# Differential attention with a routed expert before and after it: the short tile's shift of the differences from POOL to DVE

## What is computed

```python
q, k, v = rope(xn @ Wq), rope(xn @ Wk), xn @ Wv      # 16 query heads, 4 key heads
energy = einsum('bqhad,bkhad->bahqk', q, k)          # causal mask: -1e30
scores = softmax(energy / sqrt(D))
diff = scores[:, 0] - lam * scores[:, 1]             # lam: one number per head
diff = softmax(where(causal, NEG, diff))
att = einsum('bhqv,bvhd->bqhd', diff, v)
att = att * rsqrt(mean(att * att) + EPS) * rms_w * (1 - LAM_INIT)
x = x + att @ Wo
```

## Time and profile before

| | |
|---|---|
| three executions | 2122.12, 2129.94, 2130.46 us, median 2129.94 |
| profiled execution | 2123.43 us |
| its span, first to last instruction | 2121.7 us |
| PE busy | 1555.5 us (73%) |
| DVE busy | 1467.3 us (69%) |
| ACT busy | 1219.2 us (57%) |
| POOL busy | 1057.3 us (50%) |
| granted TensorE clock, mean over the span | 0.838 |

### The profile page before, as it was taken

The page is one execution under the profiler, slowest core; times in us unless marked ns, Lnnn a source line. Parts: engine busy times, 40 slices in busy tenths (PEclk is TensorE's granted clock), DMA queues, the critical chain, the costliest instruction groups (busy, mean ns, idle before and its releaser), DMA issues. The chain is left out here.

```text
span 2121.7 us, 44318 instructions
## 1 busy us (share of the span) xinstructions
PE 1555.5 (73%) x10713; PEld 1091.9 (51%) x10713; DVE 1467.3 (69%) x4351; ACT 1219.2 (57%) x3332; POOL 1057.3 (50%) x1477
## 2 busy tenths in 40 slices
PE   0579814347888888988888888888888888886521
PEld 0355402125666666666666666666666566763221
DVE  5774431127887888888888888888888776751167
ACT  0121102126887878887888887788878776761100
POOL 0220003225666667767766777767677565552200
PEclk9999956666878999899999999999999877676655
DMA  3330271111111111111111121111111100000084
GB/s 122 94 87 0 67 245 30 41 39 33 24 28 36 41 48 43 38 51 47 45 48 38 43 52 43 49 43 38 49 48 42 40 20 20 15 15 30 35 324 158
DMA packets 183784, 122.58 MB, mean 58 GB/s; under 512 B 140225, under 2 KB 140609, under 8 KB 183746
## 3 DMA queue, kind: packets, MB, share of 16 engines
q1 hardware_dynamic: 183746, 122.15, 19.6%
HBM read 57.07 MB, written 33.55 MB: 43 GB/s over the span
## 5 line engine op out<-in xcount | busy, mean ns | idle before, releaser
L1185 ACT ACTIVATE ex<-bank,nbias 128x512 f32<-128x512 f32 (+3 forms) x1024 | 527.8, 534 | 141.2 <-DVE nbias L902 140.7
L895 DVE TENSOR_REDUCE nmax<-bank 128x2 f32<-128x1024 f32 (+3 forms) x448 | 340.7, 795 | 29.9 <-PE bank L1331 29.5
L1361 PEld LDWEIGHTS bank<-vs,pr 128*128 128x128 f32 x2560 | 343.2, 210 | 17.8 <-issue 13.4
L1361 PE MATMUL bank<-vs,pr 128*128 (+1 forms) x2560 | 343.4, 286 | 7.2 <-issue 4.1
L1329 PE MATMUL bank<-ks,qs 96*128 (+2 forms) x1024 | 271.8, 342 | 95.7 <-ACT ex L1185 94.2
L1343 PE MATMUL bank<-cst,df 128*128 128x128 f32 x1280 | 274.5, 319 | 88.8 <-ACT pr L1202 88.5
L1081 POOL TENSOR_SCALAR ex<-ex,gam 128x128 f32<-128x128 f32 (+3 forms) x512 | 313.4, 623 | 0.0
L1202 ACT ACTIVATE pr<-bank 128x128 f32<-128x128 f32 (+3 forms) x512 | 233.0, 455 | 70.5 <-PE bank L1343 70.1
L927 DVE CUSTOM_DVE_ANT_0 df<-ex 128x128 f32<-128x128 f32 (+3 forms) x512 | 263.3, 529 | 9.7 <-issue 4.9
L1343 PEld LDWEIGHTS bank<-cst,df 128*128 128x128 f32 x1280 | 174.1, 171 | 117.9 <-ACT pr L1202 101.6
L1185 ACT ACTIVATION_READ_ACCUMULATOR ex<-bank,nbias 128x1 f32 x1024 | 216.6, 212 | 0.0
(11 more groups left out here) (215 smaller groups left out, 3164.0 us busy)
## 6 DMA issues: line engine op xcount, KB each, us to landing
qs<-turned SPq DMA_DIRECT2D x384, 64.0 KB, 2.2
xs<-in_x SPq DMA_DIRECT2D x64, 256.0 KB, 3.0
x_dram<-y SPq DMA_DIRECT2D x32, 256.0 KB, 3.8
b_xs<-x_dram SPq DMA_DIRECT2D x32, 256.0 KB, 2.6
x<-x_dram SPq DMA_DIRECT2D x32, 256.0 KB, 2.7
x_dram<-x SPq DMA_DIRECT2D x32, 256.0 KB, 2.0
y_dram<-scratch SPq DMA_DIRECT2D x32, 256.0 KB, 2.0
c_x<-x_dram SPq DMA_DIRECT2D x8, 1024.0 KB, 13.6
```

The lines of the kernel that those rows point to most:

```text
L895: ins = dve.tensor_reduce(nmax[:, j, i, :], energy(j, i), X, ALU.max, negate=True)
L1185: ac.activation(ex[j % 4][:, a, lo:hi], energy(j, i)[:, a, :], ACT.Exp, bias=nbias[:, j, i, a:a + 1], scale=reg, accum_out=esum[:, j, i, a ...
L1361: mm = pe.matmul(bank[:, 7, t * DV:(t + 1) * DV], pr[j % 2][:, lo + k * P:lo + (k + 1) * P], val, start=(k == 0), stop=(k == t))
```

## The change

The short tile's shift is taken from POOL's program and put into DVE's, for the same pair as the bias that DVE has just made (lag 4 for both), so a step earlier than POOL had it. In DVE's group the bias of the difference now goes ahead of gamma, and the shift comes behind gamma. POOL's mask is now the first thing of its step. PE's and ACT's programs are unchanged.

```diff
@@ DVE
+                def shift(at):
+                    j = at.j
+                    dbias_done.wait(dve, at.units(1))
+                    lo, hi = span(j, 0)
+                    dve.tensor_scalar(df[j % 4][:, lo:hi], df[j % 4][:, lo:hi], rsum[:, j, 0, 0:1],
+                                      dbias[:, j, 0:1], ALU.mult, ALU.add).then_inc(shifted_short.sem, 1)
...
-                            [(1, inv_sums), (1, gamma), (4, diff_bias), (3, difference(0))],
+                            [(1, inv_sums), (4, diff_bias), (1, gamma), (4, shift), (3, difference(0))],
@@ POOL
-                def shift(at):
-                    j = at.j
-                    dbias_done.wait(gp, at.units(1), apart_p)
-                    lo, hi = span(j, 0)
-                    gp.tensor_scalar(df[j % 4][:, lo:hi], df[j % 4][:, lo:hi], rsum[:, j, 0, 0:1],
-                                     dbias[:, j, 0:1], ALU.mult, ALU.add).then_inc(shifted_short.sem, 1)
...
-                run_bodies(gp, [[(5, shift)], [(2, mask), (2, scale)], []],
+                run_bodies(gp, [[], [(2, mask), (2, scale)], []],
```

More of the change, by code:

```diff
@@ L879, in _ @@
             def _(dve):
-                for s in (st_done, ve_done, xn_done, st2_done, ve2_done, xn2_done, rope_v, max_done, bias_done, rs_done, gam_done, diff_done, dbias_done, att_out,
+                for s in (st_done, ve_done, xn_done, st2_done, ve2_done, xn2_done, rope_v, max_done, bias_done, rs_done, gam_done, diff_done, dbias_done, shifted_short, att_out,
                           ss_done, s2_done, de_done, an_done, x2_done, lg_out):
@@ L1063, in _ @@
             def _(gp):
-                for s in (rstd_done, rstd2_done, rope_done, masked, scaled, shifted_short, sq_done, ri_done, lo_done,
+                for s in (rstd_done, rstd2_done, rope_done, masked, scaled, sq_done, ri_done, lo_done,
                           rlo_done, al_done, lo2_done):
```

## The result

| | before | after |
|---|---|---|
| median of 4 executions | 2126.03 us (2121.51 to 2130.46) | 2168.44 us (2164.25 to 2172.32) |
| profiled execution, its span | 2123.43, 2121.7 us | 2164.25, 2162.5 us |
| granted clock over the span | 0.838 | 0.83 |

The ratio is 1.0199 [1.0165, 1.0233]: slower by 2%, 42 us. The forecast was 2139 with a range of 2121 to 2159; the result lies above that range.

What follows compares the result with a forecast made beforehand. No engine was full, so a chain between engines was taken as the bound. Terms of +0.40 us in 22 turns (8.8) plus 1.0 in ten others gave +9.8 us, on the median 2139.7, stated as 2139, range 2121 to 2159.

Steps and rivals of the forecast that it cites:

- The bound: Steady attention loop: no engine is full; a chain going round between engines sets turns of 45.06 us.
- The price of the shift: On DVE: 0.31 us on 128 columns and 0.39 on 256, 88 us of busy time for 256 shifts.
- DVE's wait of 2.44 us: DVE's wait for PE at 1112.05, covering groups beside the chain; expected to fall to under 2 us.
- Term 1: DVE's group at 1085.24, on the chain: shift added, partly filling gaps; +0.10 us a turn, bounds 0 and 0.38.
- no idle time before gamma: Sign in the profile after: the bias of the difference fills DVE's 0.31 us idle before gamma at 1085.24.
- Term 2: After the power, POOL's earlier scaling meets DVE's long difference at 1091.79: +0.15 us a turn, bounds 0 and 0.59.
- Term 3: DVE's group at 1115.12, nearly on the chain: shift and one more turn-taking, +0.15 us a turn, bounds 0 and 0.75.
- Term 4: Gains from a lighter POOL at DVE's delays at 1084.35 and 1081.98: 0 us a turn, bounds -0.45 and +0.3.
- Turn-taking everywhere: Rival: every added DVE operation waits for one POOL instruction; 1.72 us a turn, 2168, halfway 2153; chance 0.15.
- The power did not block the shift: Rival claimed the opposite: DVE's shift cannot start during POOL's 2.92 us power, head norm 0.43 us later; 2154, chance 0.07.
- The lighter POOL: Rival: DVE's stalls behind POOL at 1081.98 and 1084.35 vanish, -0.45 us in 32 turns, 2116; chance 0.16.

Runs made afterwards that it cites:

- runs 5: The changed kernel with POOL's first rotary addition one place earlier, ahead of step 2's mask and scalings: 2135.09 us, ratio 1.0011.
- run 11: The changed kernel with one tiny memset (0.1 us) added on POOL ahead of the first rotary addition: 2139.11 us, ratio 1.0058.
- run 9: The kernel before with a DVE reduction over 256 constants ahead of step 2's bias of the exponentials: 2149.69 us, ratio 1.0105.
- run 2: The changed kernel with gamma ahead of the bias of the difference again, shift still on DVE: 2181.62 us, ratio 1.0209.
- run 10: The changed kernel with the bias of the exponentials in accumulator form and POOL's first rotary addition one place earlier: 2102.54 us, ratio 0.9871.
- run 12: The changed kernel unaltered, measured again on the chip of the last lot, against the kernel before: 2165.92 us, ratio 1.0179.
- run 4: The changed kernel without the short shift anywhere, DVE only raising the semaphore, and gamma's product made a comparison: 2125.12 us, ratio 0.9977.
- run 6: The changed kernel with the bias of the exponentials in the form that also writes a sum: 2102.63 us, ratio 0.9854.

## Why the prediction was wrong

- **The bound** was read rightly: a chain with turns of 45 us, on which the bias of the exponentials lies.
- **The price of the shift**, 0.31 and 0.39 us, was nearly right: 0.34 and 0.40 to 0.41 where nothing disturbs it. With its own holds the 256 shifts took 104 us, not 88. DVE's busy time rose by only 51.7 us, not by some 80, as gamma and the bias of the difference were held less. Nobody waited for the shift, and DVE's wait of 2.44 us went to 2.24 in the turn at 922.63; under 2 was expected.
- **Term 1** (+0.10) came out at its lower bound, about 0. The kernel after, ahead of the power at 922.63:
```profile
919.13 0.60 DVE L902 TENSOR_SCALAR nbias<-nmax,esc 128x4 f32<-128x4 f32 x1
...
919.73 0.12 DVE L936 SCALAR_TENSOR_TENSOR dbias<-dmax,rsum 128x2 f32<-128x2 f32 x1
920.12 0.22 DVE L915 SCALAR_TENSOR_TENSOR gam<-esum,lam,rsum 128x2 f32<-128x2 f32 x1 [0.27 <-DVE rsum L908]
920.25 0.34 DVE L944 TENSOR_SCALAR df<-df,rsum,dbias 128x128 f32<-128x128 f32 x1
920.58 0.43 DVE L927 CUSTOM_DVE_ANT_0 df<-ex 128x256 f32<-128x256 f32 x1
```
  From the end of the bias to the difference it is 0.85 us, before 0.86: the shift fits into the gaps. But an idle time before gamma stayed, 0.27 us here and 13.4 in all against 23.5; "no idle time before gamma" was wrong.
- **Term 2, shared access, is the step that failed.** I sought the new meetings only beside the operations that the change touches, and priced one of them (the long difference: 0.76 against 0.69 us, which did not reach the chain). POOL's whole list had moved by 0.73 us, up to its next real wait. The meeting that counted was between two operations which the change leaves alone, the bias at +7.84 and the rotary addition; both stood in the rows, 0.82 us apart, with the 1.32 us that the bias of the difference took where the addition held it. Its price is 1.15 us in 17 of 22 turns and 0.85 in one, not 0.15, and runs 5 and 11 remove it, with 27 us of the 37 in run 11.
- **Term 3** (+0.15) came out about right: the group at 1115.12 lies between the biases at +25.94 and +30.85, which are 4.90 us apart before and 5.03 in the turn at 922.63. A larger hold stands one step further, at +37.1 us, where the bias takes 0.84 us instead of 0.23 in 21 of 22 turns; ACT's wait for this bias ahead of the exponentials of 384 columns grew from 18.6 to 33.9 us. It did not reach the next bias: 7.16 us later in that turn, 7.15 in the turn at 1087.76 before.
- **Term 4** (0): no gain came; the bias of the place at 1084.35 takes 0.55 us in the mean of the 22 turns, against 0.49 before.
- **A term was missing**: with a longer delay on the chain, more of PE's work runs at 1.2 GHz. In the account above this makes up some 20 of the 45.8 us in the 22 turns. That is argued from comparisons; run 9 does not show it over the whole run.
- **The rivals.** Turn-taking everywhere gave 2168 at its upper end, the time that was measured, but by another way: one place at full price and the clock, not three places; that the number fits is luck. The power did not block the shift; this one lies wholly inside the power that starts at 922.63 and lasts 2.92 us:
```profile
924.75 0.41 DVE L944 TENSOR_SCALAR df<-df,rsum,dbias 128x256 f32<-128x256 f32 x1
```
  The lighter POOL did not win: by being lighter it brought the addition to the bias.

Open: what decides between two turns that are alike within 0.01 us; the exact share of the clock; why run 2 loses as much without this hold; and why the nine turns behind the steady loop got shorter.

## What to carry to other kernels

Taking work from an engine moves everything behind it, up to its next wait, and two untouched operations can meet there: lay out both engines' times over one turn, shift the one by what was removed, and look for pairs that come within a few tenths of a microsecond of each other, above all for a short operation on the chain and a long one of the other engine. If such an operation has a form that does not share the access (here the one with an accumulator), use it first: it was worth 1.0 to 1.4% in the kernel before and 2.9% in the changed one (run 10 against run 12). One meeting less is not always a gain: run 2 has not this hold and is no faster. A small delay on the chain is to be priced together with the clock it may cost.

## What was unexpected of the hardware

- A distance of 0.09 us decided over 1.15: the same bias took 1.37 us when it started at +7.84 with POOL's addition at +7.92, and 0.23 at +7.75 (run 4) or with the addition behind a memset (run 11).
- The sum-writing form of the same operation was never held: 216 to 220 ns in all 256 of run 6, with POOL's additions and scalings around it.
- The power, though 2.92 us long, held nothing: a bias in it took 0.23 us and a shift 0.41, while the rotary addition of 1.27 us held the bias ahead of it in 17 of 22 turns until it ended itself.
- Without holds of this bias, turns alternate between none and 10 us at 1.2 GHz (run 6), so the delays of this bias are not the only way to the lower clock.
